# One decoder layer on one core: bulk loads in parts, first heads by SBUF copies, half projection items, magnitudes summed by ScalarE

## What is computed

```python
def bitnet_linear(x, weight, scale_param):
    s = max(mean(abs(weight), axis=1), 1e-08)
    y = einsum('bsi,oi->bso', x, sign(weight / s[:, None]))
    return nan_to_num(y * (s * scale_param), nan=0, posinf=1e6, neginf=-1e6)
q, k, v = (bitnet_linear(layernorm(x), ...) for each)      # heads; k and v repeated 4 times
attn = softmax(q @ k.T / sqrt(16)); x = x + bitnet_linear(attn @ v, o_weight, o_scale)
def W(w, base): d = w - base; return base + mean(abs(d)) * sign(d)     # w1, w3: 1792x512, w2: 512x1792
x = x + (silu(layernorm(x) @ W1.T) * (layernorm(x) @ W3.T)) @ W2.T
```

## Time and profile before

| what | us |
|---|---|
| median of 3 runs (lowest, highest) | 1049.82 (1045.49, 1054.92) |
| the profiled execution's own time | 1054.04 |
| its span, first to last instruction | 1052.0 |
| batch 0 of the attention, 68.1 to 196.1: TensorE busy, granted clock | 114.47, 0.89 |
| batch 1, 196.1 to 301.1 | 100.28, 1.00 |
| batch 3, 405.9 to 521.8 | 100.61, 0.85 |
| feed-forward loops, 558.2 to the end | 488.45, 0.99 |

### The profile page before, as it was taken

How to read it: one execution, slowest core, us unless ns; L and a number is a source line. 1 busy time by engine, 2 the same in 40 slices (tenths; PEclk the granted TensorE clock), 3 DMA queues, 4 the chain that set the end, 5 groups by cost and what they waited for, 6 DMA issues and landing times.

```text
span 1052.0 us, 14162 instructions
## 1 busy us (share of the span) xinstructions
PE 968.0 (92%) x4770; PEld 617.9 (59%) x4770; DVE 736.5 (70%) x978; ACT 538.8 (51%) x999; POOL 293.1 (28%) x247
## 2 busy tenths in 40 slices
PE   3588989999999989898889999999999999999997
PEld 2433433344344433333357888888888888888886
DVE  6585867888888787789695558855687557864443
ACT  3426768877897889574684331332223232232221
POOL 3134767566766642210000110101111110011110
PEclk9858998999999999688999999999999999999999
DMA  4535577455754575511494000240003300130001
GB/s 149 149 127 171 158 150 227 127 146 174 224 153 115 170 224 161 179 45 32 151 303 151 12 1 1 80 148 17 0 0 120 124 0 0 45 116 1 0 0 40
DMA packets 81361, 110.24 MB, mean 105 GB/s; under 512 B 10144, under 2 KB 33696, under 8 KB 81312
## 3 DMA queue, kind: packets, MB, share of 16 engines
q1 hardware_dynamic: 79152, 108.04, 33.8%
q10 hardware_dynamic: 2160, 1.58, 0.5%
HBM read 76.29 MB, written 32.78 MB: 104 GB/s over the span
## 4 chain that ended last, share of the span: by engine, by line
PE 70%; DVE 14%; DMA 5%; issue 3%; ACT 3%; SPq 3%; POOL 2%; DVEq 0%; ACTq 0%; POOLq 0%
PE psum L1389 15%; PE psum L1390 15%; PE psum L1391 14%; DVE nmx L994 8%; PE psum L1308 7%; PE psum L1298 7%; PE psum L1282 3%; DMA q_slot<-shift 3%; DVE g_alt L963 2%; PE psum L1319 2%; PE psum L1320 2%; PE psum L1225 1%; PE psum L1226 1%; ACT probs L832 1%; SPq L454 1%
## 5 line engine op out<-in xcount | busy, mean ns | idle before, releaser
L994 DVE TENSOR_REDUCE nmx<-psum 128x2 f32<-128x1024 f32 x256 | 300.9, 1218 | 74.6 <-PE psum L1282 74.3
L832 ACT ACTIVATE probs<-psum 128x512 f32<-128x512 f32 x512 | 276.1, 604 | 77.1 <-PE psum L1298 74.9
L1298 PE MATMUL psum<-q_slot,k_slot 50*128 50x512 f32 x512 | 172.0, 492 | 16.9 <-DMA q_slot<-shift 13.0
L1389 PE MATMUL psum<-fxh,wh 128*128 128x512 f32 x448 | 175.2, 391 | 2.2 <-DVE wl L1152 2.2
L1390 PE MATMUL psum<-fxl,wh 128*128 128x512 f32 x448 | 174.9, 390 | 0.0
L1391 PE MATMUL psum<-fxh,wl 128*128 128x512 f32 x448 | 174.7, 390 | 0.0
L719 POOL CAST dh<-w2T 128x512 fp32r<-128x512 f32 (+1 forms) x56 | 50.7, 906 | 430.1 <-PE psum L1391 393.5
L1298 PEld LDWEIGHTS psum<-q_slot,k_slot 50*128 50x128 f32 x512 | 77.5, 193 | 132.1 <-ACT probs L832 85.6
L1308 PE MATMUL psum<-probs,v_slot 128*32 128x512 f32 x1024 | 146.4, 646 | 0.7 <-ACT probs L832 0.7
L1282 PE MATMUL psum<-k_slot,q_slot 48*128 48x512 f32 x512 | 115.3, 465 | 26.7 <-DVE nmx L994 24.8
L1159 DVE TENSOR_TENSOR gate<-gate,psum 128x512 f32<-128x512 f32 x56 | 38.4, 686 | 133.6 <-PE psum L1391 131.3
(11 more groups left out here) (109 smaller groups left out, 1272.7 us busy)
## 6 DMA issues: line engine op xcount, KB each, us to landing
stage<-in_L_ffn_mean_w_dram SPq DMA_DIRECT2D x84, 256.0 KB, 4.6
q_slot<-q_stack SPq DMA_DIRECT2D x64, 192.0 KB, 3.5
stage<-in_L_ffn_w_dram SPq DMA_DIRECT2D x42, 256.0 KB, 4.8
q_stack<-q_hi SPq DMA_DIRECT2D x32, 256.0 KB
weighted_values<-u_sb SPq DMA_DIRECT2D x32, 256.0 KB, 3.8
k_slot<-k_stack SPq DMA_DIRECT2D x64, 96.0 KB, 3.6
xn<-_attn_hidden_states_dram SPq DMA_DIRECT2D x4, 1024.0 KB, 6.8
q_stack<-q_lo SPq DMA_DIRECT2D x16, 256.0 KB
```

Source lines behind the costliest of these rows:

```text
L832: nc.scalar.activation(probs[kt][:, j, :], BANK[ring_bank(("score", g, kt, j))], ACT.Exp, scale=HEAD_DIM ** -0.5).then_inc(exp_ok, 1)
L994: v.tensor_reduce(column, pair, AX.X, ALU.max, negate=True).then_inc(s_max, 1)
L1298: mm(BANK[ring_bank(("score", g, kt, j))], k_slot[s][rows, kt * P:(kt + 1) * P], q_slot[s][rows, jj, :], start=True, stop=True).then_inc(t ...
L1389: mm(o, lhs_hi, rhs_hi, start=first, stop=False)
```

## The change

- **Order of items.** `ITEMS` becomes k, q, v, q, q, q. `STORED` gives the places of those that are stored. Weights of k and v are loaded and signed first.
- **First heads.** Group 0's slot is filled by 18 copies inside SBUF (`first_keys`, `first_heads`), 12 issued by SyncE and 6 by GpSimd, straight from `q_hi` and `q_lo`. Two items of batch 0, the output weights' scales, signs and transposes, and the statistics of batch 1 move in between the first 14 score pairs.
- **Factors.** The output scales are no longer stored to DRAM and loaded back spread; TensorE transposes them (`output_signs`) and ScalarE copies them.
- **Half items.** From batch 1 on an item is made in two halves of 256 token columns, in two slices one after the other. Each half stands between the slice's two score pairs, with an eviction of its own.
- **Slices.** TensorE's and ScalarE's order in a slice is turned: the first two shifted scores, a score pair, the beside work, a score pair, the other two shifted scores, then the values.
- **Differences.** GpSimd subtracts in three pieces of 128×512 in three slices; ScalarE's magnitude writes its row sum (`accum_out`) into `dsum`, and GpSimd's 14 additions to `dacc` go.
- **Loads in parts.** Tokens and residual in two DMAs each, a difference in two halves of 3 DMAs in two groups, `sums`, values, reciprocals and residual of batch 0's output projection over groups 21 to 26, the first four stage tiles one per group.
- `PROJECT_AT` is 15, 19, 23, 27 in place of 16, 20, 24, 28.

```diff
-ITEMS = (KTILE, QT, QT + 1, QT + 2, QT + 3, VTILE)
+ITEMS = (KTILE, QT, VTILE, QT + 1, QT + 2, QT + 3)
-GUARD_LAG, PRED_LAG = 1, 3
-VT_AT = 24
-DIFF_AT = tuple(range(1, 112, 8))
-SIGN_LAG, ABS_LAG, SUM_LAG = 2, 5, 8
+GUARD_LAG, PRED_LAG = 2, 4
+VT_AT = 16
+STORE_AT = (8, 12, 16, 20, 24)
+PROJECT_AT = (15, 19, 23, 27)
+DIFF_AT = tuple(range(5, 112, 8))
...
+    def first_heads(eng, part, jj, done):
+        src = (q_hi, q_hi, q_lo)[part][1]
+        for h in range(2):
+            r = HALF * h + HEAD_DIM * part
+            eng.dma_start(q_slot[0][r:r + HEAD_DIM, jj, :].bitcast(FP32),
+                          src[HEAD_DIM * (2 * h + jj):HEAD_DIM * (2 * h + jj + 1)].bitcast(FP32)).then_inc(done, 16)
...
+            elif g % 2 == 1 and g // 2 + 1 < IT:
+                load_difference(g // 2 + 1, 0)
+            elif g % 2 == 0 and g // 2 < IT:
+                load_difference(g // 2, 1)
...
-            nc.gpsimd.tensor_tensor(wn[e % 2][:], wn[e % 2][:], mn[e % 2][:], ALU.subtract).then_inc(fd_ok, 1)
-        def add_magnitude(e):
-            pool.wait_ge(fabs_ok, 3 * (e + 1))
-            nc.gpsimd.tensor_tensor(dacc[:], dacc[:], mn[e % 2][:], ALU.add).then_inc(facc_ok, 1)
+            nc.gpsimd.tensor_tensor(wn[e % 2][:, k, :], wn[e % 2][:, k, :], mn[e % 2][:, k, :], ALU.subtract).then_inc(fd_ok, 1)
...
-                    nc.scalar.activation(mn[e % 2][:, k - 3, :], wn[e % 2][:, k - 3, :], ACT.Abs).then_inc(fabs_ok, 1)
+                    nc.scalar.activation(mn[e % 2][:, k - 3, :], wn[e % 2][:, k - 3, :], ACT.Abs,
+                                         accum_out=dsum[:, k - 3, e:e + 1]).then_inc(facc_ok, 1)
...
-        for i in range(TT):
-            token_stats(1, i)
-        token_means(1)
         for nn in range(S_AHEAD):
             maxima(nn)
+            if nn in (1, 3):
+                guard(4 + nn // 2)
+                lo_item(4 + nn // 2)
+            if nn == 4:
+                weight_scales(2)
+                output_scales(slice(OT, WTILES))
             if nn == 8:
                 split_shift(0)
+            if 9 <= nn < 9 + TT:
+                token_stats(1, nn - 9)
+        token_means(1)
...
             shifted_scores(g, kt, J_ORDER[0])
+            shifted_scores(g, kt, J_ORDER[1])
             if n < S_USES:
                 scores(n)
+            if beside(g, kt):
+                beside_in(beside(g, kt))
+            if n < S_USES:
                 scores(n + 1)
-            shifted_scores(g, kt, J_ORDER[1])
             shifted_scores(g, kt, J_ORDER[2])
+            shifted_scores(g, kt, J_ORDER[3])
             if kt > 0:
                 weigh_values(g, kt - 1)
             elif g > 0:
                 weigh_values(g - 1, TT - 1)
             if kt == 1 and g < LAST_G:
                 transpose_maxima(g + 1)
-            if beside(g, kt):
-                beside_in(beside(g, kt))
-            shifted_scores(g, kt, J_ORDER[3])
```

More of the change, by code:

```diff
@@ L115, in decoder_layer @@
     fac_row = keep("fac_row", [P, 2, KT, P])
+    sums = keep("sums", [P, P])
     dtot = keep("dtot", [P, 3])
@@ L176, in decoder_layer @@
     o_alt = late("o_alt", [P, SEQ])
-    sums = late("sums", [P, P])
     st2 = late("st2", [P, TT, 6])
@@ L313, in decoder_layer, with loaded, first_keys @@
     STORES = 3 * 16
+    def loaded(g):
+        return SLOT_LOADS * (g // 4 + 1) + (FIRST_LOADS - SLOT_LOADS if g % 4 == 0 else 0)
     def stored(b, i):
         return STORES * ((5 * b + i) // Q_RING + 1)
+    def first_heads(eng, part, jj, done):
[4 more added lines that the diff above has]
+                          src[HEAD_DIM * (2 * h + jj):HEAD_DIM * (2 * h + jj + 1)].bitcast(FP32)).then_inc(done, 16)
+    def first_keys(eng, part):
+        src = (q_lo, q_hi, q_hi)[part][0]
+        for h in range(2):
+            r = HALF * h + HEAD_DIM * part
+            eng.dma_start(k_slot[0][r:r + HEAD_DIM, :].bitcast(FP32), src[0:HEAD_DIM].bitcast(FP32)).then_inc(slot_in[0], 16)
     def load_group(eng, g, s, done):
@@ L329, in beside @@
         if b == BATCH:
-            t = (at - PROJECT_AT) // PROJECT_EVERY
-            return ("project", t) if at in range(PROJECT_AT, SLICES, PROJECT_EVERY) else None
+            return ("project", PROJECT_AT.index(at)) if at in PROJECT_AT else None
         if XT_AT <= at < XT_AT + KT:
             return "xT", b, at - XT_AT
-        if at in ITEM_AT:
-            return "item", b, ITEM_AT.index(at)
+        for i in range(len(ITEMS)):
+            if 0 <= at - ITEM_AT[i] < 2:
+                return "item", b, i, at - ITEM_AT[i]
         if at == VT_AT:
@@ L368, in ring_free @@
             eng.wait_ge(xe_ok, 4 * (which[0] - 1) + which[1] + 1)
+        elif kind == "item" and which[2] == 0:
+            eng.wait_ge(y0_ok, NI * (which[0] - 1) + which[1] + 1)
         elif kind == "item":
@@ L627, in _ @@
         pool.wait_ge(slot_init, 8 + V_SLOTS)
-        pool.wait_ge(facc_init, 1)
+        pool.wait_ge(qh_ok, 2)
+        for part in range(2):
+            first_heads(nc.gpsimd, part, 1, first_in)
+        pool.wait_ge(ql_ok, 2)
+        first_heads(nc.gpsimd, 2, 1, first_in)
         pool.wait_ge(v_ok, 1)
@@ L784, in _ @@
             nc.scalar.activation(xh[:, kt, :], BANK[kt], ACT.Copy).then_inc(xh_ok, 1)
-        for i in range(NI):
-            scale_item(0, i, 4 + i % 3)
-            if i > 0:
-                hi_item(i - 1)
-        values_out(0, 7)
+        act.wait_ge(wstat_ok, 2)
+        sign_tile(QT)
+        signs_out(QT)
+        act.wait_ge(oscale_ok, 1)
+        scale_item(0, 0, 4)
+        sign_tile(QT + 1)
+        hi_item(0)
+        scale_item(0, 1, 5)
+        sign_tile(QT + 2)
+        hi_item(1)
+        scale_item(0, 2, 4)
+        signs_out(QT + 1)
+        signs_out(QT + 2)
+        sign_tile(QT + 3)
+        signs_out(QT + 3)
+        values_out(0, VT_BANK)
+        scale_item(0, 3, 5)
+        hi_item(3)
+        scale_item(0, 4, 4)
+        hi_item(4)
+        scale_item(0, 5, 5)
+        hi_item(5)
         act.wait_ge(wstat_ok, 3)
@@ L794, in _ @@
             signs_out(m)
+        for a in range(2):
+            act.wait_ge(fac_mm, a + 1)
+            nc.scalar.activation(fac_row[:, a, :, :].rearrange("p t c -> p (t c)"), BANK[FAC_BANK[a]], ACT.Copy).then_inc(fac_ok, 1)
         def beside_out(user):
@@ L805, in beside_out @@
             elif kind == "item":
-                scale_item(b, which[0], bank)
+                scale_item(b, which[0], bank, which[1])
             elif kind == "vT":
@@ L983, in _ @@
             v.tensor_tensor(xl[:, kt, :], BANK[kt], xh[:, kt, :].bitcast(FP32), ALU.subtract).then_inc(xl_ok, 1)
-        for i in range(NI):
-            guard(i)
+        guard(0)
+        lo_item(0)
+        guard(1)
+        lo_item(1)
+        guard(2)
+        guard(3)
+        lo_item(3)
         def maxima(nn):
@@ L1268, in beside_in @@
                     pe.wait_ge(xl_ok, KT * (b + 1))
[L1269 removed]
+                project_item(b, which[0], ring_bank(user), which[1])
             else:
```

364 lines of the change are left out of this document (210 added, 154 removed).

## The result

The changed kernel takes **1056.39 us** at the median of 17 runs (1049.56 to 1065.74) against 1049.82 of 17 (1042.14 to 1061.38): the ratio is **1.0069**, 95% interval 1.0041 to 1.0096. It is slower by 0.7%, within 1% and outside the forecast range. Its profiled execution took 1054.19 us (span 1052.1, mean granted clock 0.949), that of before 1054.04 (1052.0, 0.955). So the two traces are of one length and can be set against each other part by part, by the weighings that begin each group (L1421 now, L1308 before).

A forecast was written before the change was run, and what follows sets the result against it. TensorE's own work bounds the feed-forward part; before it, TensorE, VectorE and ScalarE share a ring of three banks, with late loads. Terms −1 −7 −16 −2 +3 −8 = −31 us gave 1019 us at the median, range 1002 to 1039.

The forecast's parts named there:

- Start and group 0: Up to group 1: first slice 6 us later, group 0 shorter by 7; sum −1 us, between −8 and +8.
- small copies: 18 copies at the start: no row for them; by a skill's rule the six on GpSimd's queue add some 2.5 us.
- Half items: 18 items after the first batch: a pair of slices takes 6.8 us instead of 7.67; −16 us, bounds −26 and 0.
- Projection slices ... stay as they are: Batch 3: the projection slices move by one slice and otherwise stay unchanged; no cost was charged.
- batch 3: Group 25 takes about 13 us, not 20.7, with loads spread and the inversion done earlier: −8 us, −10 to −2.
- The half difference behind the store: SyncE's queue: a half difference behind a waiting item store may cost a us per batch, inside the bounds.
- Batch 0 after group 0: Groups 1 to 7: of 9.0 us over groups 9 to 15, 7 come back and 2 stay; −7 us, 0 to −9.
- Sums on ScalarE: 42 magnitudes that also write a row sum, on a nearly full ScalarE: +3 us, 0 to +13.
- GpSimd's lock: VectorE's predicated copies held up by GpSimd: one slice per batch falls from 5.74 to 5.06 us, −2 us for three batches.
- Rival 1: ScalarE becomes the bound: half slices of 3.85 us, sums cost 10 us or more, 1042 us in all; 15%.
- Rival 3: Slower: each half item breaks the beat and costs 2.45 us, half slices average 4.26 us, 1079 us in all; 7%.
- Rival 4: Loads don't get earlier: SyncE's waits for low parts hold the shift rows as before, 1034 us in all; 13%.

The follow-up runs named there:

- e1: The changed kernel with batch 1's tokens loaded and their statistics taken ahead of the last item guards of the start: 1045.59 us, ratio 0.9963.
- e3: e1 with whole items of 512 columns in the first of the two slices, still between the score pairs: 1047.18 us, ratio 0.9997.
- e12: The kernel before with the new slice order alone; whole items, start, loads, differences and sums as before: 1058.16 us, ratio 1.0064.
- e15: The changed kernel with batch 3's slices alone in the order of the kernel before: 1046.47 us, ratio 1.0000.
- e13: e11 with all slices of batch 3 in the order of the kernel before: 1031.57 us, ratio 0.9886.
- e11: e9 with the output weight's scales two maxima earlier and the reciprocals' spreads ahead of the difference's load: 1042.46 us, ratio 0.9887.
- e6: e5 with batch 3's four projections put back after the values and ahead of the fourth score product: 1046.35 us, ratio 0.9973.
- e14: e13 with the second half of the difference's loads behind the slots' loads and ahead of the stores: 1026.15 us, ratio 0.9813.
- e4: e1 without the magnitudes' row sums on ScalarE, so the output is not the reference's: 1042.15 us, ratio 0.9955.
- e5: e1 with the second half of the difference's loads issued at the start of even groups, ahead of the shift rows: 1044.67 us, ratio 0.9957.
- e9: e1 with the second half of the difference's loads right behind the shift rows, ahead of the slots' loads and stores: 1044.38 us, ratio 0.9937.
- e10: e9 with whole items and every slice in the order of the kernel before: 1046.44 us, ratio 0.9963.
- e8: e5 with whole items and all work beside a slice back behind its values, other slices in the new order: 1080.19 us, ratio 1.0283.

## Why the prediction was wrong, point by point

- **The step that failed: "Start and group 0", sum −1.** The first scores at 40 (38.85) and group 0's fall by 7 (7.0) were right. The first weighing was put at 74 and came at 91.8. I had listed the statistics of batch 1 as 3 us of VectorE's work and had not asked who waits for them. GpSimd does (power and four norms, 9.4 us), and slice 0's transposes wait for GpSimd, in the middle of TensorE's in-order program. Moved from ahead of the maxima to behind the tenth to thirteenth, they put 11 us of idle time and a half-speed clock on the path. e1 undid it and got 13 us back. The term as a whole measured +10.6 (17.6 − 7.0) where −1 was forecast, outside even its −8 to +8. The small copies were no part of it: the six on GpSimd's queue took 3.3 us to issue, with VectorE at work beside them, and landed in 2.1 us at the median, as SyncE's did in 1.9 to 2.3.
- **Half items, −16.** Mechanism right, size off. Half slices took 3.63 us on average (3.4 taken), a pair 7.26 (6.8). With the groups around them, batch 2, the one without a stall, gained 3 us instead of 5.3: the groups with the items −3.6 in batch 1 and −2.9 in batch 2, and the other groups give some back, as a slice with the copy of weighted sums takes 3.21 in place of 2.96. e3 and e12 showed that it is mostly the new place of the item, not the halving. I had counted place and halving as one edit.
- **"Projection slices ... stay as they are"** (batch 3, −8) failed. Group 25 gave 9.5, more than forecast, but the slice order is the projections' order too. The projection's bank is wanted by the next slice's first score product rather than its second, and VectorE's multiplication isn't done by then (2.1 and 2.2 us). e15 against the changed kernel puts this at 7 us by the ratios (3.6 in the two profiles); e13's profile against e11's at 11.5. That bank mechanism is read from the trace; e6, which was to test it by itself, made a mixture of orders. That the order as a whole costs here is shown by e15.
- **The half difference behind the store: "may cost a us per batch".** The place was right, the price not: 11 us from issue to landing, GpSimd, norm and transposes in a chain, 3.30 us of idle time and a lowered clock (0.97 over the batch, 1.00 before), and group 15 at 18.4 us where e14's took 12.2. In e1, e4 and e15 it appeared too, in one or two batches each, not always the same. e5, e9 and e14 moved the same load through three places of the queue, and each time what stood behind it was late; only ahead of the stores and behind the slots' loads (e14) was no load late.
- **Batch 0 after group 0, −7.** Groups 1 to 7 fell by 7.6, but they also hold a third of the terms for items, lock and sums, so 12 were forecast for them. By the prediction's own measure, set against batch 2 because batch 1 now has a stall, they took 9.3 us more than groups 17 to 23 before (101.2 and 91.9), and 4.8 more now (93.6 and 88.8). So 4.5 of the 7 came, and not 2 but 4.8 us are left.
- **Sums on ScalarE, +3.** e4's slices give an estimate of 1.8 us for all 42; its times don't settle it (3.4 us by the medians, 0.8 by the ratios). **GpSimd's lock, −2.** No run had this alone. In the old order the slice that met a long addition fell from 5.74 us to e10's 4.82, but the plain slices around it grew, and groups 9 to 12 took 58.2 us against 58.1, groups 16 to 20 took 70.2 in both. So as far as the runs show, the term gave nothing in that order. The predicated copies averaged 0.902 us.
- **The rivals.** None was it. Rival 1 has ScalarE bound; its busy time rose to 91.6 us but half evictions and sums cost what the forecast had. Rival 3 (a break's price paid twice) would need half slices of 4.26. Rival 4 (loads no earlier) lies nearest in kind, but group 0 and batch 0 did gain. The case that happened, a result put behind other work with two engines waiting for it, was no rival at all.

In all, by stretch, forecast and measured (the terms for items, lock and sums, −15, are spread evenly over batches 0 to 2):

| stretch | forecast, us | measured, us |
|---|---|---|
| start and group 0 | −1 | +10.6 |
| groups 1 to 7 | −12 | −7.6 |
| batch 1 | −5 | +3.5 |
| batch 2 | −5 | −3.0 |
| batch 3 | −8 | −3.0 |
| from there to the end | 0 | −0.4 |

The start misses by 12 of the 31 us, batch 1 with its stall by 8 or 9, batch 3 by 5, groups 1 to 7 by 4 and batch 2 by 2.

## What to carry to other kernels

When an instruction is moved down one engine's program, follow its result through every engine to the first in-order instruction that needs it, and add up those durations; the moved instruction's own cost is the least of it. Take the work behind such a wait at the lower clock that the rows behind waits show. A change of order within a repeated slice is a change for everything that shares the slice and its ring of banks: price it per kind of slice, and choose the order per stretch (e13). When a big transfer stands in a queue with small urgent ones, try its place ahead of what waits long (stores) and behind what is wanted soon (shift rows, slots): three places of one load gave 1044 to 1046 us (e1, e5, e9), and the fourth, e14, a median 5 us under the same kernel with the third (e13), though with overlapping intervals.

## What the runs showed of the hardware that was not expected

- An ACTIVATE with an accumulator output shows as a second instruction, ACTIVATION_READ_ACCUMULATOR, of 0.208 us (42 of them). Left out in e4, it shortened the last of each three slices with magnitudes by 0.09 us and most of the others not at all.
- Idle time is paid a second time in the work behind it. After e9's wait of 3.65 us the four score products took 1.22 us where 0.74 is usual, and the slice behind them 4.02 instead of 2.82. In e10 and e9 the same work of groups 26 to 30, in its two orders, took 70.6 us at a clock of 0.98 and 79.9 at 0.87: 4.4 us more of idle time and 4.9 us more of busy time.
- Two orders of a slice that each run well (2.61 us for a plain slice in either) ran badly when alternated: e8's item slices took 5.3 and 6.3 us, against 4.8 in the one order and 4.4 in the other, and the kernel 1080 us.
- Issuing two of the difference's loads on SyncE's queue took 2.83 us at 286.14, behind the item's stores; in e5, at 388.63, it took 0.93, and in e9, right behind the shift rows, 0.88 to 1.19 each time. The queue's own time is part of the delay.
